# The causal mask of an attention kernel: from a matrix product into the sum to an addition by VectorE in PSUM

## The reference

```python
k = jnp.einsum('ihd,bpd->biph', W_K, x)
q = jnp.einsum('ihd,bpd->biph', W_Q, x)
v = jnp.einsum('ihd,bpd->biph', W_V, x)
scores = jnp.einsum('biph,biqh->biqp', k, q)
mask = jnp.tril(jnp.ones((pos, pos), dtype=x.dtype))
masked = scores * mask - jnp.float32(10000000000.0) * (1.0 - mask)
attn = jax.nn.softmax(masked / jnp.sqrt(jnp.float32(d_head)), axis=-1)
z = jnp.einsum('biqp,biph->biqh', attn, v)
...
x = x + attention(layernorm(x))
x = x + experts(layernorm(x))
```

## Time and profile before

| | |
|---|---|
| median of three runs | 1378.24 us |
| lowest and highest | 1376.92, 1378.34 us |
| the profiled execution, first to last instruction | 1405.0 us |
| TensorE busy | 1328.9 us, 95% |
| VectorE busy | 905.6 us, 64% |
| ScalarE busy | 722.3 us, 51% |
| GpSimd busy | 571.1 us, 41% |
| granted TensorE clock, mean | 0.990 |

### The profile page before, as it was taken

One profiled execution on the slowest core, in us unless ns is written; L12 is line 12 of the kernel. 1 busy time (PEld: TensorE's weight loads), 2 busy tenths in 40 slices (PEclk: granted clock), 3 DMA queues, 4 the chain that ended last, 5 costly groups with the idle time before them and its releaser, 6 DMA issues.

```text
span 1405.0 us, 28535 instructions
## 1 busy us (share of the span) xinstructions
PE 1328.9 (95%) x8578; PEld 1171.3 (83%) x8578; DVE 905.6 (64%) x1875; ACT 722.3 (51%) x1688; POOL 571.1 (41%) x587
## 2 busy tenths in 40 slices
PE   5999999999999899999999999999889997989998
PEld 4888888888888787888778888888779887978886
DVE  5667666666667878687886666666776632345536
ACT  2655555555555555554445555555455553545443
POOL 5535535355232223213043635441003664546554
PEclk9999999999999999999999999999999998999999
DMA  3253544525533000000001201020459996899963
GB/s 118 83 173 105 188 164 133 172 97 183 164 135 102 19 20 16 16 16 20 12 31 60 66 27 68 34 86 0 151 202 311 368 337 237 307 363 378 302 200 116
DMA packets 128246, 195.98 MB, mean 139 GB/s; under 512 B 10400, under 2 KB 99744, under 8 KB 128160
## 3 DMA queue, kind: packets, MB, share of 16 engines
q1 hardware_dynamic: 64752, 110.04, 23.4%
q10 hardware_dynamic: 51120, 51.26, 10.9%
q0 software_dynamic: 12288, 33.57, 6.8%
HBM read 107.79 MB, written 87.03 MB: 139 GB/s over the span
## 4 chain that ended last, share of the span: by engine, by line
PE 82%; DVE 7%; issue 3%; ACT 3%; DMA 3%; another core or an unknown queue 1%; SPq 1%; ACTq 0%; POOL 0%; POOLq 0%; DVEq 0%
PE ps_s L782 9%; PE ps_t L841 8%; PE ps_s L784 8%; PE ps_s L783 8%; PE ps_x L782 6%; PE ps_x L783 6%; PE ps_x L784 6%; PE ps_z L782 5%; PE ps_z L784 5%; PE ps_z L783 5%; PE ps_t L1006 3%; PE ps_z L1006 3%; PE ps_s L975 2%; PE ps_t L782 2%; PE ps_t L783 2%
## 5 line engine op out<-in xcount | busy, mean ns | idle before, releaser
L1116 ACT ACTIVATE prob<-ps_s,neg_max 128x128 f32<-128x128 f32 (+7 forms) x256 | 189.4, 741 | 256.3 <-DVE neg_max L1312 252.1
L1327 DVE TENSOR_TENSOR pT_lo<-ps_t,pT_hi 128x512 fp32r<-128x512 f32 (+2 forms) x320 | 189.4, 603 | 104.9 <-ACT pT_hi L1132 101.3
L1132 ACT ACTIVATE pT_hi<-ps_t 128x512 fp32r<-128x512 f32 (+2 forms) x320 | 161.4, 533 | 94.8 <-PE ps_t L841 92.1
L1312 DVE TENSOR_REDUCE neg_max<-ps_s 128x1 f32<-128x128 f32 (+7 forms) x256 | 186.8, 748 | 14.0 <-PE ps_s L784 11.5
L679 POOL DMA_INDIRECT xs<-xn,slots x128 | 127.7, 997 | 134.8 <-PE ps_z L1006 67.6
L841 PE MATMUL ps_t<-ident,prob 128*128 128x128 f32 x1152 | 170.8, 274 | 9.4 <-ACT prob L1116 4.2
L841 PEld LDWEIGHTS ps_t<-ident,prob 128*128 128x128 f32 x1152 | 136.7, 140 | 33.1 <-DVE pT_lo L1327 5.7
L782 PE MATMUL ps_s<-k_hi,q_hi 128*128 128x512 f32 (+2 forms) x384 | 154.7, 403 | 0.0
L1524 DVE TENSOR_TENSOR h<-sg,ps_s 128x256 f32<-128x256 f32 x112 | 46.9, 418 | 155.9 <-ACT sg L1166 103.9
L782 PE MATMUL ps_s<-ring,a_hi 128*128 x384 | 125.5, 327 | 14.3 <-SPq L530 11.9
L784 PE MATMUL ps_s<-k_hi,q_lo 128*128 128x512 f32 (+2 forms) x384 | 133.7, 348 | 0.0
(11 more groups left out here) (306 smaller groups left out, 3682.9 us busy)
## 6 DMA issues: line engine op xcount, KB each, us to landing
ring<-ws SPq DMA_DIRECT2D x56, 512.0 KB
xs<-taken SPq DMA_DIRECT2D x16, 1536.0 KB, 9.8
xq<-xs ACTq DMA_DIRECT2D x48, 512.0 KB
xs<-yq ACTq DMA_DIRECT2D x48, 512.0 KB
ws<-split_to SPq DMA_DIRECT2D x34, 512.0 KB, 3.1
raw<-experts_dram SPq DMA_DIRECT2D x34, 256.0 KB, 3.4
raw_a<-w_a_dram SPq DMA_DIRECT2D x15, 512.0 KB, 4.4
ring_down<-experts_dram SPq DMA_DIRECT2D x56, 128.0 KB
```

What stands on the lines that cost most here:

```text
L1116: act.activation(prob[c][:, j, 0:width(r)], ps_s[r % 2][:, 0:width(r)], ACT.Exp, bias=neg_max[:, r:r + 1], accum_out=row_sum[:, c, j:j + 1 ...
L1132: act.activation(to, ps_t[m % 2][:, j * P:], ACT.Copy).then_inc(s_hi, 1)
L1312: dve.tensor_reduce(neg_max[:, r:r + 1], ps_s[r % 2][:, 0:width(r)], AX.X, ALU.max, negate=True).then_inc(s_max, 1)
L1327: dve.tensor_tensor(lo, ps_t[m % 2][:, j * P:], hi.bitcast(F32), ALU.subtract).then_inc(s_bank_free, 1)
```

## The change

The product of identity and causal block and its two bf16 constants go; a bf16 `mask` with the same values stays, and VectorE adds it to the diagonal block in PSUM, waits for that addition, and takes the maximum. The row of five tiles is placed 128 columns further right in its two banks, so that it divides into products of 384 and 256 columns. The constants are counted anew, VectorE waits for six of them at its start, and some buffers get other sizes or places.

```diff
+def row_from(r):
+    return P if r == BC else 0
+
+def row_parts(r):
+    cut = NQ - row_from(r)
+    return [(0, max(width(r), 2 * P))] if r < BC else [(0, cut), (cut, max(width(r), cut + 2 * P))]
...
-    ident, ident_bf = sb("ident", [P, P]), sb("ident_bf", [P, P], BF16)
-    causal = sb("causal", [P, P], BF16)
+    ident = sb("ident", [P, P])
+    mask = sb("mask", [P, P], BF16)
...
-    number_int = sb("number_int", [1, TILES], mybir.dt.int32)[:, :]
+    number_int = flat(chosen).bitcast(mybir.dt.int32)[0:1, 0:TILES]
...
-        split_to = [sb(f"split_to{n}", [P, 2 * GU + 2 * D], F32R, attention) for n in range(2)]
-        raw = [sb(f"raw{n}", [P, GU + D], F32, attention) for n in range(2)]
+        split_to = [sb(f"split_to{n}", [P, 2 * GU], F32R, attention) for n in range(2)]
+        raw = [sb(f"raw{n}", [P, GU], F32, attention) for n in range(2)]
+        sb("below_routing", [P, 3 * S + (NT + 1) * E + S - 6 * GU], F32, attention)
...
-    CONSTS = 25 + WORD
+    CONSTS = 23 + WORD
...
-        pool.memset(ident_bf[:, :], 0.0).then_inc(s_const, 1)
-        pool.memset(causal[:, :], 0.0).then_inc(s_const, 1)
-        pool.wait_ge(s_const, 5)
-        for m in (ident, ident_bf):
-            pool.affine_select(out=m[:, :], in_=m[:, :], compare_op=ALU.not_equal, fill=1.0,
-                               base=0, pattern=[[-1, P]], channel_multiplier=1).then_inc(s_const, 1)
-        pool.affine_select(out=causal[:, :], in_=causal[:, :], compare_op=ALU.is_ge, fill=MASKED,
+        pool.memset(mask[:, :], 0.0).then_inc(s_const, 1)
+        pool.wait_ge(s_const, 4)
+        pool.affine_select(out=ident[:, :], in_=ident[:, :], compare_op=ALU.not_equal, fill=1.0,
+                           base=0, pattern=[[-1, P]], channel_multiplier=1).then_inc(s_const, 1)
+        pool.affine_select(out=mask[:, :], in_=mask[:, :], compare_op=ALU.is_ge, fill=MASKED,
                            base=0, pattern=[[-1, P]], channel_multiplier=1).then_inc(s_const, 1)
...
-        pe.wait_ge(s_const, 8)
+        pe.wait_ge(s_const, 6)
...
-            pe.matmul(to[:, r * P:(r + 1) * P], ident_bf[:, :], causal[:, :], start=True, stop=False,
-                      skip_group_check=True)
-            for k0 in range(0, width(r), NQ):
-                k1 = max(min(width(r), k0 + NQ), k0 + 2 * P)
-                diagonal = k0 <= r * P < k1
-                last = three(to[:, k0:k1], q_hi[a][:, q], q_lo[a][:, q], k_hi[a][:, k0:k1],
-                             k_lo[a][:, k0:k1], not diagonal, True, diagonal)
+            for k0, k1 in row_parts(r):
+                at = slice(row_from(r) + k0, row_from(r) + k1)
+                last = three(to[:, at], q_hi[a][:, q], q_lo[a][:, q], k_hi[a][:, k0:k1],
+                             k_lo[a][:, k0:k1], True, True)
...
-            act.activation(prob[c][:, j, 0:width(r)], ps_s[r % 2][:, 0:width(r)], ACT.Exp,
-                           bias=neg_max[:, r:r + 1],
+            act.activation(prob[c][:, j, 0:width(r)], ps_s[r % 2][:, row_from(r):row_from(r) + width(r)],
+                           ACT.Exp, bias=neg_max[:, r:r + 1],
...
             dve.wait_ge(s_scores, row + 1)
-            dve.tensor_reduce(neg_max[:, r:r + 1], ps_s[r % 2][:, 0:width(r)], AX.X, ALU.max,
+            at = row_from(r) + width(r)
+            diagonal = ps_s[r % 2][:, at - P:at]
+            dve.tensor_tensor(diagonal, diagonal, mask[:, :], ALU.add).then_inc(s_masked, 1)
+            dve.wait_ge(s_masked, row + 1)
+            dve.tensor_reduce(neg_max[:, r:r + 1], ps_s[r % 2][:, row_from(r):at], AX.X, ALU.max,
                               negate=True).then_inc(s_max, 1)
...
+        dve.wait_ge(s_const, 6)
         for kind, k, n, m in walk(START):
```

More of the change, by code:

```diff
@@ L425, in build @@
     s_bank, s_hi, s_bank_free = sem("bank"), sem("pT_hi"), sem("bank_free")
-    s_pv = sem("pv")
+    s_pv, s_masked = sem("pv"), sem("masked")
     s_x, s_x_hi, s_x_free = sem("x"), sem("x_hi"), sem("x_free")
@@ L646, in _ @@
         pool.iota(thr_int, pattern=[[P, NT]], base=0, channel_multiplier=0).then_inc(s_const, 1)
-        pool.wait_ge(s_const, 18 + 1 + WORD)
+        pool.wait_ge(s_const, 16 + 1 + WORD)
         pool.tensor_copy(number[:, :], number_int).then_inc(s_const, 1)
```

## The result

The changed kernel takes 1401.14 us (median of four runs, 1397.88 to 1404.2), the kernel before on the same chip 1378.29 us (1376.92 to 1379.32). The ratio is 1.0169, with a 95% interval from 1.015 to 1.0188: 22.9 us slower. The forecast was 1390 us and slower. The side was right, the loss was twice as large as forecast: above the 1383 to 1399 us that I had given the likeliest case, inside the wide range of 1366 to 1403.

A forecast was written before the change was run, and what follows sets the result against it. TensorE, busy 95% of the span, bounds the kernel. Plain pairs 4.4, four late ones 1.1, woven pairs 2.9, 1.5 and twice 0.5, opening with last pair 0.8: +11.7 us on 1378.2, 1390 us; 8 in 10 within 1366 to 1403.

The forecast's parts named there:

- The price of the addition: On VectorE, 256 additions ahead of the maxima: 0.286 us each, the maximum starting 0.04 us behind each.
- c: VectorE's added time per row of scores, addition plus lost overlap: 0.32 us, 82 us in all.
- Rival (a): Faster: the maximum overlaps the addition, or the PSUM write ends sooner; 0.21 us a row, 1373 us; chance 0.17.
- Rival (d): Worse: the addition takes 0.36 us, 0.40 a row, or VectorE fills in the woven pairs; 1401, up to 1408 us; chance 0.15.
- its second case: VectorE fills in the pairs with other work woven in; up to 1408 us if these get more.
- The chain of the first head: Plain pair, four additions between VectorE and ScalarE: chain 1.10 us later, transposes 0.83 later, TensorE idle over 1 us.
- The second head: Plain pair: chain 0.87 us later, TensorE waits 0.5 us before the transposes; this head comes to -0.11 us.
- TensorE's saving: Mask products 0.115 us each, 29.4 us, and the five-tile row 5.6 us: 35.0 us together, 2.19 a pair.
- The plain pairs: Eleven pairs of heads without woven work: +0.4 us each, 4.4; four of them +1.1 more for transposes already waiting.
- The woven pairs: Four pairs with other work woven in: +2.9 us at 649.00, +1.5 the one before, +0.5 each near 449.70.
- The last pair: End of the attention, taken together with the first rows: +0.8 us.
- The experts and the layout: Experts keep their time and start 12 us later; smaller buffers move the same bytes, at nothing.

The follow-up runs named there:

- e6: The changed kernel with the addition written to an unread SBUF tile and no wait before the maximum, mask left out of the result: 1375.22 us, ratio 0.9982.
- e8: The changed kernel with the addition only for rows of five to eight tiles, mask product for the others: 1399.97 us, ratio 1.0159.
- e2: The kernel before with only the five-tile row divided as 384 + 256, mask still by product: 1374.08 us, ratio 0.997.
- e5: The changed kernel without the addition and its wait, so no mask on the diagonal blocks: 1355.02 us, ratio 0.9844.
- e1: The kernel before run once more, unedited, for a second trace: 1377.35 us, ratio 0.9996.
- e12: The changed kernel with one routing step of pair nine moved behind the first head's transposes: 1398.96 us, ratio 1.0134.
- e3: The kernel before with only the changed kernel's buffer sizes and places: 1377.86 us, ratio 1.0005.
- e4: The changed kernel with the buffer layout of the kernel before: 1399.48 us, ratio 1.0167.
- e11: The changed kernel with the addition only for short rows (one to four tiles) of the eleven plain pairs, mask products elsewhere: 1366.72 us, ratio 0.9908.
- e7: The changed kernel with the addition only for rows of one to four tiles, mask product for the others: 1372.59 us, ratio 0.9965.
- e9: The changed kernel with the addition only for rows of five and six tiles, mask product for the others: 1385.57 us, ratio 1.0052.

## Why the prediction was right and where it was not

**The price of the addition: right.** 0.286 us forecast, 0.288 measured; maximum 0.04 behind it, 0.03 to 0.04 measured; c = 0.32 a row, 0.33 from addition to maximum in the pair shown. Writing to PSUM is no cheaper or dearer than e6's write to a tile in SBUF (280 ns). Rival (a), the maximum overlapping the addition, did not come. e6 is that rival built: c = 0.20, and 1375.2 us, where (a) had 1373. Rival (d) had named 1401 us, the measured time, but for c = 0.40 in every row; c was 0.33, and that its number was met is chance. Nearer is its second case, VectorE filling in the woven pairs: that is where the loss lies, though VectorE's share of pair ten only went from 86% to 88%. On the section "The DRAIN you can't avoid" of the Trainium skill's "VectorE: DVE Perf Modes", by which a semaphore between chained instructions costs nothing extra (measured there on eight tensor_copy): the runs disagree for an addition and a maximum with operands in PSUM. With a wait on the instruction just ahead the next one starts 0.03 to 0.04 us after its end, without it 0.08 before, and the kernels differ by 26 us, part of it by what the later VectorE then runs into (e6).

**The chain of the first head: right.** Counted from the start of a plain pair (154.60 before, 155.30 after), the exponential's last part came at 164.21 - 154.60 = 9.61 and now comes at 166.12 - 155.30 = 10.82, 1.21 later for 1.10 forecast. The transposes' weight loads went from 10.12 to 11.06, 0.94 later for 0.83. TensorE idles 1.22 us there, put down to the exponential, where I had asked for over 1 us. e8 shows that this is the long rows' doing. VectorE's busy share of the pair rose to 75%, for about 76% forecast.

**The second head: too dear.** By the earlier trace rows I let its chain come 0.87 us later and TensorE wait 0.5. Its transposes' weight loads went from 39.53 to 39.76 us into the pair (194.13 and 195.06), and the wait is 0.20 us, of the weight loads alone: the products behind one another have no gap there. I had taken off only the 0.41 us that VectorE idled before its fourth maximum. There is a second slack ahead of the third: VectorE's split q_lo waits for ScalarE's q_hi, and this waited for TensorE. The exponential just ahead of q_hi came 1.28 us later than before, q_hi itself 1.05 (32.98 to 34.03 us into the pair). From z_hi ahead of this chain, 0.65 us later in its pair than before (27.75 to 28.40), to the last exponential, 1.21 later (37.30 to 38.51), the chain of the second head lost 0.56 us.

**TensorE's saving: too high.** The five-tile row is worth its 0.175 us in a plain pair (e2). The mask products are worth 1.43 us for 16 in a plain pair (58.63 in e2, 57.20 in e5), 0.089 each and not 0.115, a quarter less. Over the whole kernel the 35.0 us were 22.4 (e5). I had read the step on rows that follow other products of this kind. Seven of the 16 rows follow transposes, and there the first product is slow in any case. TensorE of the changed kernel, a product of 384 columns behind transposes, then behind scores:

```profile
155.30 0.42 PE L792 MATMUL ps_s<-k_hi,q_hi 128*128 128x384 f32 x1
155.55 0.34 PE L793 MATMUL ps_s<-k_lo,q_hi 128*128 128x384 f32 x1
...
159.94 0.33 PE L792 MATMUL ps_s<-k_hi,q_hi 128*128 128x384 f32 x1
160.11 0.34 PE L793 MATMUL ps_s<-k_lo,q_hi 128*128 128x384 f32 x1
```

The step is 0.25 us in the first case and 0.17 in the second. By that the mask product ahead had covered most of the difference; no run shows it by itself.

**The plain pairs: +0.4 forecast, +0.10 measured**, and the eleven with the opening 1.3 us where my sum had 5.5 and some of its 0.8. The second head is most of the difference. 1.1 us of the 5.5 was the wait of the earlier trace rows, which e1 doesn't have.

**The woven pairs: the term that failed.** The sum had "the pair at 649.00 ... +2.9. The one before it: +1.5, halfway. The two near 449.70 ...: +0.5 each", 5.4 us in all; they took 14.8. Pair ten, the one at 649.00, was not far off (3.6); the others were priced at a third of what they took or less, and pair nine grew most, not pair ten as I had said. I priced them by how busy VectorE is, which is a share, and not by their chains. TensorE's waits over the four pairs, first in the second trace of before:

```profile
PE ps_t L841 <- DVE pT_lo L1327: 2.9, 2, 2.1
PE ps_t L841 <- ACT prob L1116: 2.1, 3, 1.4
```

then after:

```profile
PE ps_t L848 <- ACT prob L1123: 12.4, 8, 3.7
PE ps_t L848 <- DVE pT_lo L1338: 5.0, 3, 2.8
```

The wait for the exponential, the same that bounds the first head of a plain pair, comes eight times in the four pairs, and its sum grows by 10.3 us. Of the 12.4 us, 3.7 are one stall in pair nine, behind the meeting with GpSimd that is told in the last section and that I had not thought of; in e12, without it, the sum is 8.3 us in seven waits. In a plain pair the second head's chain had slack; in a woven one it has little. ScalarE in pair ten, two instructions around the second head's long rows, second trace of before (pair from 648.67 on):

```profile
679.54 0.60 ACT L1110 ACTIVATE k_hi<-ps_x 128x512 fp32r<-128x512 f32 x1 [0.38 <-PE ps_x L784]
...
691.57 1.12 ACT L1116 ACTIVATE prob<-ps_s,neg_max 128x1024 f32<-128x1024 f32 x1 [1.17 <-DVE neg_max L1312]
```

and after (pair from 660.50 on):

```profile
692.84 0.60 ACT L1117 ACTIVATE k_hi<-ps_x 128x512 fp32r<-128x512 f32 x1
...
706.20 1.11 ACT L1123 ACTIVATE prob<-ps_s,neg_max 128x1024 f32<-128x1024 f32 x1 [1.50 <-DVE neg_max L1323]
```

The first comes 1.47 us later in its pair (30.87 and 32.34), the second 2.80 (42.90 and 45.70): this chain lost 1.33 us, four times c and a little, where the plain pair's second head lost 0.56. The first heads of both lose nearly all of it (1.21 and 1.26), and in pair ten none of it is given back before the next head (at z_hi it is 1.47 us, in the plain pair 0.65). e5 says the same from the other side: in pairs nine and ten hardly any of the mask product's saving is kept. The last pair, in which I had forecast under 0.8 us with the opening, took 2.5. TensorE already idled 5.1 of its 59.0 us before the change, which points to the chains here too; no run tests that pair by itself.

**The experts and the layout: right.** The experts start later and keep their time within 0.8 us; e3 and e4 put the layout at nothing. The difference between the profiled execution of 1405.0 us and the median, which I carried over, touched nothing here: of the 28.2 us between the two traces of the kernel before, 24.7 us are in the experts (383.2 us there in the first trace from the first down product to the last, 358.5 in the second) and 3.3 in the four late pairs.

The mechanism was thus in the main the one forecast: a fixed delay c in each step of the chain VectorE, ScalarE, VectorE, ScalarE. Two errors of size ran against each other, too much for the plain pairs and much too little for the woven ones, and the second was larger; that the total still fell inside the wide range owes something to the first. The woven pairs also hold what the forecast had no term for, GpSimd's hold on VectorE in pair nine and the clock, both in the last section.

## What to carry to other kernels

Work taken off the busiest engine is worth at most what it costs there at its own place, and work put on another engine is priced by the chain that it enters, at each place once for its duration and once for the overlap that its dependence takes away; slack in a chain can be spent once. Price each stage by its own chain rather than by how busy an engine is. Where a change has places that gain and places that lose, make it only at the first: e11 did so and was faster than both kernels.

## What the runs showed of the hardware beyond that

**VectorE held up by GpSimd.** In pair nine of the changed kernel an addition of two tiles of SBUF, 128x256, took 2.45 us. The timeline of that place, VectorE and GpSimd:

```profile
597.78 2.41 POOL L607 TENSOR_TENSOR v_lo<-v_raw,v_hi 128x1024 fp32r<-128x1024 f32 x1
...
598.01 2.45 DVE L1378 TENSOR_TENSOR biased<-score,bias_bc 128x256 f32<-128x256 f32 x1
...
604.65 0.75 PE L848 MATMUL ps_t<-ident,prob 128*128 128x128 f32 x3 [3.68 <-ACT prob L1123]
```

In the second trace of before it starts 0.24 us ahead of the same GpSimd instruction, while the one before that, v_hi, still runs (to 591.69):

```profile
591.53 0.44 DVE L1367 TENSOR_TENSOR biased<-score,bias_bc 128x256 f32<-128x256 f32 x1
...
591.77 2.46 POOL L597 TENSOR_TENSOR v_lo<-v_raw,v_hi 128x1024 fp32r<-128x1024 f32 x1
```

It costs 0.44 us there and 2.45 when it starts behind GpSimd's v_lo. Each time it ends 0.27 or 0.28 us behind the GpSimd instruction that was running when it started (597.78 + 2.41 against 598.01 + 2.45, and 591.69 against 591.53 + 0.44). In e7 it started 0.32 us before the end of v_hi and took 0.60 us. The additions of the change had pushed it from the one case to the other; the same happened in e4, e8 and e9. e12 moved it away from GpSimd: 0.42 us, and the pair 2.9 us shorter, half of its growth of 5.9. The additions of the mask, with one operand in PSUM, kept their 271 to 300 ns throughout. The Trainium skill, "SBUF — State Buffer", section "Who interferes with whom", says that a VectorE instruction with two SBUF inputs contends with a GpSimd instruction that reads SBUF, that one with a single SBUF input does not unless it runs in a mode that uses both ports, and that the order of issue decides who is blocked. The traces agree for the two kinds of addition. A tensor_scalar with one SBUF tensor (L1290, 128x256) did take up to 2.51 us for its usual 0.41, in pairs seven and eight beside GpSimd's v_lo, and as long in both traces of the kernel before; whether it ran in such a mode no trace says.

**The clock behind a stall.** Windows of 2 us of the changed kernel behind that idle time:

```profile
602.00:604.00 2.00, 0.00 (x0) 0.00 (x0) 1.23 (x2) 1.64 (x3) 0.00 (x0) 1.00 0.22 66
604.00:606.00 2.00, 1.35 (x7) 1.39 (x8) 1.10 (x4) 1.51 (x5) 0.00 (x0) 0.70 0.00 0
606.00:608.00 2.00, 2.00 (x9) 1.81 (x8) 1.93 (x8) 1.43 (x3) 0.00 (x0) 0.50 0.00 0
608.00:610.00 2.00, 2.00 (x14) 1.77 (x14) 1.13 (x3) 0.60 (x1) 0.00 (x0) 0.95 0.00 0
```

TensorE had idled 3.68 us; the granted clock then fell to 0.50, the 1.2 GHz level. Against full speed the last three windows lack 2 x (0.30 + 0.50 + 0.05) = 1.7 us of TensorE's clock, an estimate of the most that the fall cost on top of the stall. In e12, where that stall is gone, the clock stays at 1.00 there. A long stall of TensorE can thus be paid for twice. Such falls are in every trace in pair seven (0.93 to 0.97 over the pair); the changed kernel has them in pairs eight and nine too. I could not separate them by an experiment from the waits that bring them. A rough size comes from e5, whose TensorE runs the same 1497 instructions in the four woven pairs: the changed kernel's is busy 250.1 us there and e5's 244.1. A plain pair has 0.65 us of such a difference (57.85 and 57.20) at a clock of 1.00 in both, so 6.0 - 4 x 0.65 = 3.4 us are left for the lower clock, an estimate. How much of that the length of the pairs shows, and how much of the spread of the four runs from 1397.9 to 1404.2 is the clock's, stays open.
